# A two-layer kernel's ternary feed-forward written as one chain over inner tiles

## The reference, cut to what matters

```
def act_quant(x):
    scale = 127.0 / jnp.clip(jnp.max(jnp.abs(x), axis=-1, keepdims=True), 1e-05)
    return jnp.clip(jnp.round(x * scale), -128, 127) / scale

def weight_quant(w):
    scale = 1.0 / jnp.clip(jnp.mean(jnp.abs(w)), 1e-05)
    return jnp.clip(jnp.round(w * scale), -1, 1) / scale

h = act_quant(x) @ weight_quant(w1).T          # 512 -> 2048
h = depthwise_conv1d(h, conv_w) + conv_b       # 3 taps along the tokens
h = silu(h)
y = act_quant(h) @ weight_quant(w2).T          # 2048 -> 512, scale per token over all 2048
```

## Time and profile before

| | us |
|---|---|
| median of 3 runs (lowest, highest) | 2036.26 (2032.58, 2038.72) |
| the profiled execution | 2037.65 |
| its span | 2035.5 |
| PE busy over the span | 1678.0 (82%) |
| DVE busy | 1348.6 (66%) |
| ACT busy | 1109.4 (55%) |
| POOL busy | 1090.0 (54%) |
| granted PE clock, mean | 0.916 |

### The profile page before, as it was taken

How to read it: one execution, slowest core, us unless ns; L and a number is a source line. 1 busy time by engine, 2 the same in 40 slices (tenths; PEclk the granted TensorE clock), 3 DMA queues, 4 the chain that set the end, 5 groups by cost and what they waited for, 6 DMA issues and landing times. The chain is left out here.

```text
span 2035.5 us, 31756 instructions
## 1 busy us (share of the span) xinstructions
PE 1678.0 (82%) x8819; PEld 723.8 (36%) x8834; DVE 1348.6 (66%) x1931; ACT 1109.4 (55%) x1817; POOL 1090.0 (54%) x760
## 2 busy tenths in 40 slices
PE   5978636778887785489999999999999985699998
PEld 2434312333333332233333333333333321344443
DVE  5988777888888865465657575757565662664653
ACT  3444257676655771345556565656565642656563
POOL 3555405787666783335556555555565642454442
PEclk9888858899988988689999999999999997899999
DMA  8121000000000000310101010101011101010001
GB/s 305 43 72 52 1 0 0 1 0 0 0 0 0 1 1 0 112 56 26 53 25 53 25 52 25 53 25 52 26 50 28 36 13 44 18 42 21 35 27 42
DMA packets 60453, 72.06 MB, mean 35 GB/s; under 512 B 14416, under 2 KB 40016, under 8 KB 59856
## 3 DMA queue, kind: packets, MB, share of 16 engines
q1 hardware_dynamic: 57520, 62.62, 9.7%
q10 hardware_dynamic: 2848, 8.52, 1.1%
HBM read 37.40 MB, written 8.39 MB: 22 GB/s over the span
## 5 line engine op out<-in xcount | busy, mean ns | idle before, releaser
L1212 DVE TENSOR_REDUCE s_mx<-bank 128x1 f32<-128x512 f32 x512 | 334.6, 676 | 245.3 <-PE bank L1317 242.8
L1138 ACT ACTIVATE s_E<-bank 128x512 f32<-128x512 f32 x512 | 293.2, 594 | 232.1 <-PE bank L1331 202.2
L1062 POOL TENSOR_TENSOR s_E<-s_E 128x1024 f32<-128x1024 f32 x128 | 299.9, 2353 | 159.4 <-PE bank L1339 132.7
L842 PE MATMUL bank<-f_zh,f_w1q 128*128 128x512 f16 x512 | 203.8, 398 | 53.8 <-DVE f_y L717 45.5
L1317 PE MATMUL bank<-s_KA,s_QA 96*128 96x512 f16 x512 | 194.9, 391 | 23.9 <-DVE s_mx L1212 15.0
L1331 PE MATMUL bank<-s_QA,s_KA 97*128 97x512 f16 x512 | 199.8, 392 | 11.6 <-ACT s_E L1138 7.9
L843 PE MATMUL bank<-f_zl,f_w1q 128*128 128x512 f16 x512 | 203.3, 397 | 0.0
L555 POOL TENSOR_TENSOR f_y<-f_y,f_t 128x511 f32<-128x511 f32 x128 | 171.3, 1346 | 53.3 <-DVE f_y L717 52.7
L549 POOL TENSOR_TENSOR w1raw<-w1raw,f_s2b 128x512 f32<-128x512 f32 x123 | 164.7, 1357 | 43.3 <-ACT f_s2b L640 43.3
L1055 POOL TENSOR_TENSOR s_qkl<-s_qkf,s_qkh 128x512 f16<-128x512 f32 x64 | 74.0, 1156 | 192.1 <-ACT s_qkh L1116 192.1
L865 PE MATMUL bank<-f_w2q,w2raw 128*128 128x512 bf16 x497 | 125.5, 409 | 30.8 <-DVE w2raw L709 22.3
(11 more groups left out here) (217 smaller groups left out, 3884.7 us busy)
## 6 DMA issues: line engine op xcount, KB each, us to landing
X<-in_x SPq DMA_DIRECT2D x8, 1024.0 KB, 7.1
s_QA<-s_qkh SPq DMA_DIRECT2D x256, 32.0 KB, 1.8
s_KA<-s_qkh SPq DMA_DIRECT2D x256, 32.0 KB, 1.8
out_x<-X SPq DMA_DIRECT2D x8, 1024.0 KB, 4.2
a_cf<-in_ctx SPq DMA_DIRECT2D x8, 768.0 KB, 4.7
s_cf<-in_ctx SPq DMA_DIRECT2D x8, 768.0 KB, 4.7
w1raw<-in_w ACTq DMA_DIRECT2D x1, 4096.0 KB, 13.2
w2raw<-in_w ACTq DMA_DIRECT2D x1, 4096.0 KB, 28.4
```

The source lines that it names most:

```text
L842: e.matmul(HB[j % NHB][:, :], w1q[:, cols], zh[:, c, :], start=(c == 0), stop=False)
L1062: e.tensor_tensor(into, into, other, ALU.add).then_inc(s_sum.sem, 1)
L1138: e.activation(E[:, SLOT[k] + h, :], SC[u % 2][:, :], ACT.Exp, scale=1.0 / float(np.sqrt(DH)))\
L1212: e.tensor_reduce(mx[:, q, h:h + 1], MX[q % 2][:, :], AX.X, ALU.max).then_inc(s_red.sem, 1)
```

## The change

The stage's loops are rewritten. The second product goes inner tile by inner tile (`products`): each rounded tile is multiplied into four banks, one for each token tile, which stay open over the whole batch. The first product has three banks left, and the chunks of the next batch, the maxima and the spread share the last one, AB. The chain runs over step boundaries: in step `b` the slots j = 0 to 5 finish the second product of `b-2`, and slots 8 to 15 start that of `b-1`. The order of inner tiles in the second product begins at tile 4 and ends with tiles 0 to 3 (ORDER), and tiles 0 to 3 of odd batches have a second place (`others`), as has the split input (`spare`), both in the space of the raw w2. The last part of the maxima, the scales and the spread of `b-1` lie in slots 2 to 5 of step `b`. POOL multiplies from slot 5 on. Normalising, token scales, rescaling and the chunks of `b+1` lie in slots 0 to 13. Six tiles are rounded on ACT instead of four. The running maximum lies in `top` in SBUF instead of a bank. The loop runs over pairs of batches (2 to 5), and the tail's 16 multiplies are split 6 on POOL, 10 on DVE, with the products following tile by tile.

```diff
-        zh, zl = sb("zh", [P, KD, S], F16), sb("zl", [P, KD, S], F16)
...
+        others = w2raw[:, half:half + 2 * quarter].rearrange("p (j s i) -> p j s i", s=S, i=2)
...
+        spare = w2raw[:, half + 2 * quarter:2 * half].bitcast(F16).rearrange("p (h c s) -> p h c s", h=2, s=S)
+        zh0, zl0 = sb("zh", [P, KD, S], F16), sb("zl", [P, KD, S], F16)
+        zh = lambda odd, c: spare[:, 0, c, :] if odd else zh0[:, c, :]
+        zl = lambda odd, c: spare[:, 1, c, :] if odd else zl0[:, c, :]
...
+        ORDER = tuple(range(4, KF)) + tuple(range(4))
+        BY_ACT = (1, 3, 6, 9, 12, 14)
+        TAIL_SHARED = (2, 4, 7, 9, 12, 14)
...
-        T, HB, PK, AB, OB = banks[0:2], banks[2:4] + banks[0:2], banks[4], banks[5], banks[6:8]
+        HB, AB, OB = banks[0:3], banks[3], banks[4:8]
...
+        s_l2, s_res = tally("l2", KF + TT - 1), tally("res", TT)
...
+        def g(odd, j):
+            return (others if odd and j < 4 else pairs)[:, j // 2, :, j % 2]
+
+        on_act = lambda r: r in BY_ACT
+        nact = lambda r: sum(i < r for i in BY_ACT)
+        hb = lambda odd, j: HB[(j + odd) % NHB][:, :]
+        first_bank = lambda c: banks[3 - c % 2]
...
+        def steps(e, step):
+
+            step(0, 0, False, False, True, True)
+            step(1, 1, True, False, True, True)
+            with e.Fori(1, B // 2 - 1) as pair:
+                step(pair * 2, 0, True, True, True, True)
+                step(pair * 2 + 1, 1, True, True, True, True)
+            step(B - 2, 0, True, True, True, False)
+            step(B - 1, 1, True, True, False, False)
 
...
-            def step(b, first, ahead):
+            def step(b, odd, has_a, has_c, ahead, ahead2):
+                if ahead:
+                    ln_p(e, b + 1)
                 for j in range(KF):
-                    if not first and j + EARLY < KF:
-                        scaled(b - 1, j + EARLY)
+                    if has_c and j < 3:
+                        scaled(b - 2, odd, 13 + j)
+                    if has_a and j >= 7:
+                        scaled(b - 1, 1 - odd, j - 3)
                     tap(b, j)
-                if ahead > 1:
-                    ln_p(e, b + 2)
-                for j in range(EARLY):
-                    scaled(b, j)
+                    if has_a and j in (5, 6):
+                        scaled(b - 1, 1 - odd, 2 * (j - 5))
+                        scaled(b - 1, 1 - odd, 2 * (j - 5) + 1)
 
             ln_p(e, 0)
-            ln_p(e, 1)
-            steps(step, e)
-            for j in range(EARLY, SHARED):
-                scaled(B - 1, j)
+            steps(e, step)
...
+            def raised(b, odd, r):
+
+                s_u.wait(e, b, r + 1)
+                o = g(odd, ORDER[r])
+                e.activation(o, o, ACT.Identity, bias=round_c[:, 0:1]).then_inc(s_up.sem, 1)
+
+            def whole(b, odd, r):
+
+                if r < 12:
+                    s_l2.wait(e, b - 1, r + 1)
+                else:
+                    s_res.wait(e, b, 0)
+                s_up.wait(e, b, nact(r + 1))
+                e.activation(gq[:, r, :], g(odd, ORDER[r]), ACT.Identity, bias=nround[:, 0:1]).then_inc(s_ga.sem, 1)
...
+            def spread_out(b):
...
+            def step(b, odd, has_a, has_c, ahead, ahead2):
+                for j in range(KF):
+                    if j < 4:
+                        mine = [(b - 2, odd, 12 + j)] if has_c else []
+                    elif j in (6, 7):
+                        mine = [(b - 1, 1 - odd, 2 * (j - 6) + 1)] if has_a else []
+                    elif j >= 8:
+                        mine = [(b - 1, 1 - odd, j - 4)] if has_a else []
+                    else:
+                        mine = []
+                    mine = [m for m in mine if on_act(m[2])]
+                    for m in mine:
+                        raised(*m)
+                    middle(b, odd, j)
+                    late(b, odd, j)
+                    for m in mine:
+                        whole(*m)
+                    if j >= 2:
+                        silu(b, odd, j - 2, has_c if j < 6 else has_a)
+                    elif has_a:
+                        silu(b - 1, 1 - odd, KF - 2 + j, has_c)
+                    if has_a and j == 5:
+                        spread_out(b - 1)
+                    if ahead and j in (6, 7):
+                        rescaled(b + 1, 2 * (j - 6))
+                        rescaled(b + 1, 2 * (j - 6) + 1)
+                    if ahead and 10 <= j < 10 + KD:
+                        high(b + 1, 1 - odd, j - 10, AB)
 
             e.wait_ge(s_c, 2)
...
+                    s_aT.wait(e, b, 0)
...
+                    e.tensor_tensor(top[:, :], top[:, :], part[:, k % 2, :], ALU.max).then_inc(s_pk.sem, 1)
...
+            def residual(b, odd, q):
...
+            def step(b, odd, has_a, has_c, ahead, ahead2):
...
+                    taps(b, odd, j)
+                    if has_c and j < 4 and not on_act(12 + j):
+                        whole(b - 2, odd, 12 + j)
+                    if has_a and j in (6, 7):
+                        whole(b - 1, 1 - odd, 2 * (j - 6))
+                    if has_a and j >= 8 and not on_act(j - 4):
+                        whole(b - 1, 1 - odd, j - 4)
+                    if ahead and j < 2:
+                        normalise(e, b + 1, (2 * j, 2 * j + 1))
+                    if has_a and j == 2:
+                        largest(b - 1, 1 - odd, 3)
+                    if has_a and j == 3:
+                        scales(b - 1)
+                        back(b - 1, 1 - odd)
+                    if ahead and j == 4:
+                        token_scales(b + 1)
+                    if has_c and j in (6, 7):
+                        residual(b - 2, odd, 2 * (j - 6))
+                        residual(b - 2, odd, 2 * (j - 6) + 1)
+                    if ahead and j in (8, 9):
+                        rescale(b + 1, 2 * (j - 8))
+                        rescale(b + 1, 2 * (j - 8) + 1)
+                    if ahead and 10 <= j < 10 + KD:
+                        low(b + 1, 1 - odd, j - 10, AB)
+                    if j in (8, 12, 14):
+                        largest(b, odd, (8, 12, 14).index(j))
+                    if ahead2 and j in (13, 15):
+                        stats(e, b + 2, j - 13)
+                        stats(e, b + 2, j - 12)
+                    if ahead2 and j == KF - 1:
+                        moments(e, b + 2)
+
+            for q in range(TT):
+                stats(e, 0, q)
...
+            mine = [r for r in range(KF) if r not in TAIL_SHARED]
+            for n, r in enumerate(mine):
+                o = g(1, ORDER[r])
+                e.tensor_tensor(o, o, s2b[:, :], ALU.mult).then_inc(s_tm, 1)
+                if n:
+                    e.wait_ge(s_tm, n)
+                    e.tensor_scalar(gq[:, mine[n - 1], :], g(1, ORDER[mine[n - 1]]), ROUND, ROUND,
+                                    ALU.add, ALU.subtract).then_inc(s_gq.sem, 1)
...
+            def linear1(b, odd, j):
+                if j == 0:
+                    s_zl.wait(e, b, KD)
+                s_c1.wait(e, b, j + 1 - NHB if odd or j >= NHB else min(j - 1, 0))
+                for c in range(KD):
+                    cols = slice(c * F + j * P, c * F + (j + 1) * P)
+                    e.matmul(hb(odd, j), w1q[:, cols], zh(odd, c), start=(c == 0), stop=False)
+                    last = e.matmul(hb(odd, j), w1q[:, cols], zl(odd, c), start=False, stop=(c == KD - 1))
+                last.then_inc(s_h.sem, 1)
...
+            def products(r):
+                for q in range(TT):
+                    last = e.matmul(OB[q][:, :], gq[:, r, q * P:(q + 1) * P], w2q[:, ORDER[r] * D:(ORDER[r] + 1) * D],
+                                    start=(r == 0), stop=(r == KF - 1))
+                    if r == KF - 1 or q == TT - 1:
+                        last.then_inc(s_l2.sem, 1)
+
+            def linear2(b, r):
+                if r == 0:
+                    s_res.wait(e, b, 0)
+                rounded(e, b, r)
+                products(r)
+
+            def transposed(b, c):
+                if c == 0:
+                    s_r2.wait(e, b, TT)
+                    s_s2b.wait(e, b - 1, 0)
+                s_zl.wait(e, b, c)
+                chunk(e, b, c, AB)
+
+            def step(b, odd, has_a, has_c, ahead, ahead2):
                 for j in range(KF):
-                    last = e.matmul(OB[q % 2][:, :], gq[:, j, q * P:(q + 1) * P], w2q[:, j * D:(j + 1) * D],
-                                    start=(j == 0), stop=(j == KF - 1))
-                last.then_inc(s_o.sem, 1)
-
-            def transposed(b, c):
-                s_r2.wait(e, b, TT)
-                if c < 2:
-                    taken(b - 1, KF - 1 + c)
+                    if ahead and 10 <= j < 10 + KD:
+                        transposed(b + 1, j - 10)
+                    linear1(b, odd, j)
+                    if has_c and j < 6:
+                        linear2(b - 2, 10 + j)
```

(80 more changed lines are left out.)

237 lines of the change are left out of this document (80 added, 157 removed).

## The result

The changed kernel takes 2187.58 us (median of 4 runs, 2185.73 to 2191.65) against 2037.49 (4 runs): a ratio of 1.074 (95%: 1.071 to 1.077), 150 us slower, where +109 was forecast. The profiled execution took 2186.16, its span 2184.3. The loss lies in the feed-forward: the stage, from the first tap to the end of the last residual, went from 508.0 us to 661.3 (299.86 to 961.16), +153, and the spans differ by 149 (1.5 us came off ahead of the stage, 3 behind it).

The account below looks back on a forecast made before the run. No engine was full, DVE nearest; queue order would lengthen a middle step from 61.4 to 80.5 us. Steps and tail summed to 617.3 against 508.0, +109.3, so about 2146 us; own range 2105 to 2185, whole range 2080 to 2200.

Parts of the forecast that it names:

- the two chains: Waits through the engines' ordered queues in slots 5 to 8 (17.0 us) and slots 10 to 13 (26.0 us).
- rival 4: PE's clock: all tiles of slots 10 to 13 at half clock, 56 us more, near 2200; chance 16%.
- the signs that were named: Chunks 5.5 to 7 us apart, DVE waiting 6 and 5 before taps 6 and 7, clock under 0.92, lower DVE share.
- A: Slots 15 and 0 to 3 of a middle step, `taps(15)` through scales and diagonals: 18.8 us.
- B: After the diagonals in a middle step: `back`, `taps(4)`, `token_scales`, `taps(5)`: 4.7 us, to 23.5.
- C: Slots 5 to 8: taps wait for POOL's `scaled` and ACT's `raised`: 17.0 us, DVE having 4.7 of work.
- D: Slots 8 and 9: two taps, two `whole`, four `rescale`, `largest(0)`: 10.0 us, to 50.5.
- E: Slots 10 to 13: four chunks share one bank, each waiting for the last one's `low`: 26.0 us.
- F: End of a middle step: `taps(14)`, `whole`, `largest(2)`, `max`: 4.0 us, to 80.5.
- Rival 3: Only one of the two chains costs as worked out, a step near 70: near 2083; chance 14%.
- Rival 1: Queues run ahead, both chains hide, DVE bounds at about 55 a step: about 1982; chance 7%.
- The rule on banks: Rotating banks for the chunks' transposes: by it alone 1.9 us a chunk, which gives nothing to pay.

Follow-up runs that it names:

- Experiments 2 and 5: Each against the changed kernel: 2, ACT's `raised` behind `late` in slots 6 and 7, 2164.98 us; 5, POOL's `scaled` ahead of `tap` in slots 5 and 6, 2155.72 us.
- Experiment 4: Changed kernel plus ten matmuls with overwritten results on PE ahead of chunks 1 to 3: 2170.67 us, ratio 1.066 to the kernel before.
- Experiment 8: Changed kernel reordered: chunks behind tiles 11 to 14, their `high` and `low` first in slot, `raised` later, `scaled` ahead of `tap`; 2037.44 us, 1.0014 of the kernel before.

## Why the prediction was right, and where its sizes were off

The direction, the two chains and the bound by order were right; the forecast of +109 fell 44 short of the stage's +153. The measured 2187.6 lies inside the whole range (2080 to 2200) but 3 us outside the forecast's own (2105 to 2185), and nearer to rival 4's 2200 than to 2146. Of the signs that were named, DVE's waits before taps 6 and 7 (6.0 and 4.4), the lower clock (0.82) and DVE's lower share (57% of the step, where it was 84%) came as said; the chunks stand 7.3 to 8.4 us apart, wider than the 5.5 to 7 that were named.

**A and B**, 18.8 + 4.7 = 23.5 forecast: 23.8 measured in step 3 (to the end of `taps(5)`). The `max` into `top`, taken at 0.7 between 0.7 and 1.8, took 0.69 to 0.72: the choice between the bounds was right.

**C**, 17.0: 16.8. The wait before tap 6 was 6.0 (forecast 6.1), the next two taps came after 6.8 and 3.8 us (7.1 and 3.8). Experiments 2 and 5 take one link out each and gain 23 and 32 us.

**D**, 10.0: 9.9.

**E**, 26.0: 30.6. This is the term that was mis-sized. The bound by `low` is as forecast, and the fourth chunk with what follows took 7.4 against 7.5. But the first three of the four tiles ran for the most part at half clock, 0.43 us a matmul, so that slots took 8.4, 7.3 and 7.3 against 7.1, 5.7 and 5.7. The forecast had a tile at 1.9 and 2.2 us there, full clock with a share at half; at half it is 3.4. Rival 4, at 16%, had this mechanism, and its price (8 a step, 56 in all) was too high: over the seven steps E took 28 us more than forecast. Forecast and rival 4 were not exclusive: the chain itself makes PE idle, and in it the granted clock falls. Experiment 4 shows the link, for with PE busy the slot is 5.65 and E as a whole 27.1 against the forecast's 26.0.

**F**, 4.0: 4.0. The step is 85.0 against 80.5.

**The sum.** Steps 2 to 5: 341.5 against 322.0, of which E is 17.5 (29.6 to 31.2 a step). Step 0: 59.5 against 53.0, step 1 78.4 against 75.1 and step 6 81.2 against 79.3, in each of which taps 9 to 13 stand 5.7 to 9.6 us apart, as in a middle step; E is 6.6, 2.3 and 1.8 over its forecast in them. Step 7: 58.1 against 53. There I had the second product at nothing, in gaps. Its first tile waited 11.4 us for the residual and began at 893.55, and `middle` waited 5.2 behind it. In the middle steps PE waits as long (13.5), but DVE has its rescaling to do meanwhile, which step 7 lacks; that this is the reason is argued and not tested. The tail: 42.5 against 34.9. 3.1 came ahead of POOL's first multiply, where PE has 12 products (5.2 us, 0.43 each) in front of the spread. The rest, 4.5, is PE's: DVE was done with its ten pairs in 16.1 (forecast 16.5), but the products had not kept up, and DVE waited 5.9 us for them where I had put 0.9. Together 19.5 + 6.5 + 3.3 + 1.9 + 5.1 + 7.6 = 44.

**The rivals.** Rival 3 (one chain cheaper) is out. Rival 1 said that without the chains a step would take 55 and the kernel 1982. Experiment 8 made that kernel, and its step takes 61.9: the price was wrong by 7 a step. Contention was in that 55, and DVE's busy time, 52.4, stayed under it; what the rival left out is the 9.5 us in which DVE still waits, about as much as before (9.9).

What the saved roundings give is paid beside POOL. Rescaling and normalising, which met POOL's instructions less before, now stand beside them. Before, and in experiment 8:

```profile
L697 DVE TENSOR_SCALAR f_z<-f_z,f_rs 128x512 f32<-128x512 f32 x4 | 3.2, 810 | 0.0
L111 DVE TENSOR_SCALAR f_z<-X,f_mv,f_rstd 128x512 f32 x4 | 1.9, 542 | 0.0
...
L752 DVE TENSOR_SCALAR f_z<-f_z,f_rs 128x512 f32<-128x512 f32 x4 | 5.8, 1497 | 0.0
L111 DVE TENSOR_SCALAR f_z<-X,f_mv,f_rstd 128x512 f32 x4 | 5.6, 1446 | 1.1 <-POOL f_rstd L125 1.1
```

The same eight instructions take 6.3 us more. In the tail after, a multiply of 1.78 us stands beside POOL's and one of 0.68 just behind its end at 946.30; a rounding has 1.52 and 0.41. The Trainium skill, SBUF — State Buffer, Who interferes with whom, says that a DVE instruction with two SBUF inputs contends with a GpSimd instruction that reads SBUF, and that in DVE's two-port modes, which a `tensor_scalar` can enter when its operands allow it, whoever issues first holds the shared ports for its whole instruction. The lengths in these rows agree; which of the two came first wasn't looked at. So DVE's work can't be counted by its lengths alone.

Of the 9.5 us, 5.1 are waits for `late`, 1.8 for `high` and 1.1 for `ln_p`; whether a further order of the queues would take them away was not tried. What bounds the step of 61.9 stays open.

**The rule on banks.** The forecast set the Trainium skill's rule (Perfetto Trace Analysis, Matmuls) on rotating banks beside the filler between the groups. Experiment 8 keeps the one bank and passes the chunks of a middle step through it 3.0 to 4.3 us apart, where the change took 7.3 to 8.4 for the same: here the filler decides. That doesn't speak against a second bank: whether one would have helped with the order of the change as it was, no run shows.

## What to carry to other kernels

When work of another chain is interleaved into an in-order queue, follow each resource that it waits for round all engines: if the piece that frees it stands behind the main work of the same slot, slots run one after the other, and full overlap becomes a sum. Put the freeing instructions ahead of the main work in each queue and the requesting one a slot after its data is due, before judging the idea. And compare the best case with the bound first: here DVE had 51.5 us of work in 61.4, and with the chains gone its waits for `late` fell from 8.0 to 5.1 us while other waits took their place. Last, try each part of a change by itself: the tail alone gained 9.7 us, and in the whole it stayed hidden behind a loss.
